# The softmax over the neighbours, computed batch by batch inside the neighbour sum

## What is computed

```
lrelu = lambda h: leaky_relu(h, 0.2)
h = lrelu(_bn(feat @ W1.T, g1, b1))
h = lrelu(_bn(h @ W2.T, g2, b2))
h = lrelu(_bn(h @ W3.T, g3, b3))           # one channel
att = softmax(h[..., 0], axis=-1)          # over K = 30 neighbours
agg = einsum('bnkc,bnk->bnc', x.T[bidx, idx], att)
return x + agg.T
```

## Time and profile before

| | us |
|---|---|
| median of 3 runs | 6674.75 |
| fastest and slowest run | 6666.72, 6677.72 |
| the profiled execution, its own time | 6667.89 |
| its span, first to last instruction | 6665.9 |
| busy: TensorE, VectorE, ScalarE, GpSimd | 5685.7, 5886.1, 4461.5, 3249.3 |
| attention and neighbours | to about 5100 |
| third layer's end to the last softmax operation | 5373.5 to 5422.5 |
| start-up of the neighbour sum | 5422.5 to 5453.2 |
| neighbour sum | 5453.2 to 6665.9 |

### The profile page before, as it was taken

The page is one execution under the profiler, slowest core; times in us unless marked ns, Lnnn a source line. Parts: engine busy times, 40 slices in busy tenths (PEclk is TensorE's granted clock), DMA queues, the critical chain, the costliest instruction groups (busy, mean ns, idle before and its releaser), DMA issues. The chain is left out here.

```text
span 6665.9 us, 228315 instructions
## 1 busy us (share of the span) xinstructions
PE 5685.7 (85%) x83284; PEld 3456.0 (52%) x83284; DVE 5886.1 (88%) x8332; ACT 4461.5 (67%) x17049; POOL 3249.3 (49%) x3279
## 2 busy tenths in 40 slices
PE   7888888888888888888888888888839949999998
PEld 3454545455555545545554555555423337677776
DVE  7999999999999999999999999999946588777776
ACT  7787878787787878787877878788822533333333
POOL 3455655555555555555655555555550023333332
PEclk9999988898888999898898998998859979999999
DMA  2333333233333333333233333333241013333332
GB/s 48 89 97 85 93 91 91 84 91 87 100 92 91 97 85 94 91 90 91 85 92 102 91 91 92 93 91 90 80 118 35 0 38 90 90 83 89 87 84 78
DMA packets 633780, 564.50 MB, mean 85 GB/s; under 512 B 535517, under 2 KB 557277, under 8 KB 598653
## 3 DMA queue, kind: packets, MB, share of 16 engines
q1 hardware_dynamic: 632572, 548.75, 29.1%
HBM read 380.55 MB, written 67.24 MB: 67 GB/s over the span
## 5 line engine op out<-in xcount | busy, mean ns | idle before, releaser
L703 ACT ACTIVATE prob<-SC,row_max 128x64 f32<-128x64 f32 x6144 | 1835.3, 327 | 671.7 <-DVE row_max L1032 664.8
L817 POOL TENSOR_TENSOR prob<-prob,row_rec 128x512 f32<-128x512 f32 x768 | 829.9, 1081 | 1897.7 <-DVE row_rec L1040 1897.1
L703 ACT ACTIVATION_READ_ACCUMULATOR prob<-SC,row_max 128x1 f32 x6144 | 1349.0, 220 | 0.0
L1024 DVE FIND_INDEX8 nbr<-top,dist 128x8 uint16<-128x1024 f32 x1024 | 1235.8, 1220 | 0.0
L1017 DVE MAX8 top<-dist 128x8 f32<-128x1024 f32 x1024 | 1194.1, 1207 | 12.6 <-DVE y_b L1055 10.3
L610 PE MATMUL PT<-ident,prob 128*128 128x128 f32 x3072 | 516.1, 295 | 573.9 <-ACT prob_t L710 563.2
L610 PEld LDWEIGHTS PT<-ident,prob 128*128 128x128 f32 x3072 | 383.6, 151 | 1076.8 <-issue 1033.2
L589 PE MATMUL SC<-k_bd,q_t 128*64 128x256 f32 x6144 | 935.8, 430 | 0.0
L1019 DVE MATCH_REPLACE8 dist<-top,dist 128x1024 f32<-128x1024 f32 x768 | 925.2, 1210 | 0.0
L1816 DVE TENSOR_TENSOR d_oh_a<-lo,iota_a 128x4096 bf16<-128x4096 bf16 x256 | 584.4, 2293 | 255.2 <-PE DM L1667 254.8
L1708 ACT ACTIVATE dense<-DM 128x512 f32<-128x512 f32 x512 | 305.6, 597 | 746.3 <-PE DM L1667 746.1
(11 more groups left out here) (194 smaller groups left out, 9538.6 us busy)
## 6 DMA issues: line engine op xcount, KB each, us to landing
low_all<-low_scratch SPq DMA_DIRECT2D x256, 1024.0 KB, 4.9
k_bd<-k_t SPq DMA_DIRECT2D x3072, 16.0 KB, 1.9
placed<-compact SPq DMA_DIRECT2D x256, 192.0 KB, 3.7
ctx<-in_ctx SPq DMA_DIRECT2D x32, 512.0 KB, 4.0
mask<-in_mask SPq DMA_DIRECT2D x32, 512.0 KB, 7.8
xb<-in_x SPq DMA_DIRECT2D x32, 512.0 KB, 4.3
x_scratch<-xb SPq DMA_DIRECT2D x32, 512.0 KB, 4.7
y_scratch<-y_b SPq DMA_DIRECT2D x32, 512.0 KB, 6.6
```

What stands on the lines that cost most here:

```text
L703: last = act.activation(prob[:, s % 4, g * CHUNK:(g + 1) * CHUNK], SC[:, s % 2, g * CHUNK:(g + 1) * CHUNK], ACT.Exp, bias=row_max[:, s % 2 ...
L817: pool.tensor_tensor(pr, pr, row_rec[:, r % 2, :].unsqueeze(2).to_broadcast([128, 8, CHUNK]), ALU.mult).then_inc(normed, 1)
L1024: last = dve.max_index(nbr[:, uu % BPB, t, k * 8:(k + 1) * 8], best, row)
```

## The change

The softmax leaves `batch_norms`. There GpSimd now lays out the rows, a pair of neighbours at a time behind each transpose of the third layer, without gain and shift; `att` has rows of 30 and `gain3` and `shift3` are kept for the next part. In `neighbour_sum` each batch's rows get their softmax one batch ahead: ScalarE's copy after x = 1 applies gain and shift; VectorE does the leaky ReLU, the maximum and the subtraction at the end of slot 1 (`exponents`); ScalarE does the exponential after x = 5 (`powers`); VectorE does the sum, the reciprocal and the multiply in slot 3, ahead of the transpose (`weights`). In the start-up the memsets of `placed` go behind the transpose (VectorE) and behind the split (GpSimd), and VectorE waits for the constants later.

```
 batch_norms, GpSimd, behind inv2:
+                if n == 1:
+                    by_row = att[:, :, :].rearrange("p (b t) k -> p b t k", t=NT)
+                    for m in range(PAIRS_K):
+                        pool.wait_ge(z3_turned, m + 1)
+                        pool.tensor_copy(by_row[:, :, :, 2 * m:2 * m + 2], S[:, 0, 2 * m:2 * m + 2, :].rearrange("p k (t b) -> p b t k", t=NT)).then_inc(laid_out, 1)
 batch_norms, ScalarE and VectorE: the four-part softmax is taken out
-            for x in range(PARTS_S):
...
+            wait(dve, "gain3")
 neighbour_sum, ScalarE:
-              act.activation(at_n[:, :].rearrange("p (n k) -> p n k", k=KP), keep["att"][:, bass.ds(b(NT), NT), :],
-                               ACT.Identity).then_inc(copied_in, 1)
+              act.activation(at_n[:, :, 0:K], keep["att"][:, bass.ds(b(NT), NT), :], ACT.Identity, scale=keep["gain3"][:, 0:1],
+                               bias=keep["shift3"][:, 0:1]).then_inc(copied_in, 1)
+            def powers(b):
+                act.wait_ge(lowered, START + b(1, 1))
+                act.activation(at_n[:, :, 0:K], at_n[:, :, 0:K], ACT.Exp).then_inc(powered, 1)
...
+                    if x == 5 and not is_last(i, u):
+                        powers(counter(i, u + 1))
 neighbour_sum, GpSimd:
             pool.wait_ge(consts_in, START + 16 * len(CONSTS))
+            split_weights(counter(0, 0), 0, False)
             pool.memset(placed[:, 1, :, :, :, :], 0.0).then_inc(cleared[1], 1)
-            split_weights(counter(0, 0), 0, False)
 neighbour_sum, VectorE:
+            def exponents(b):
+                own, wide = at_n[:, :, 0:K], [128, NT, K]
+                dve.wait_ge(copied_in, START + b(1, 1))
+                dve.scalar_tensor_tensor(own, own, SLOPE, own, ALU.mult, ALU.max).then_inc(leaky, 1)
+                dve.wait_ge(leaky, START + b(1, 1))
+                dve.tensor_reduce(top[:, :], own, AX.X, ALU.max).then_inc(highest, 1)
+                dve.wait_ge(highest, START + b(1, 1))
+                dve.tensor_tensor(own, own, top[:, :].unsqueeze(2).to_broadcast(wide), ALU.subtract).then_inc(lowered, 1)
             def weights(b):
-                dve.wait_ge(copied_in, START + b(1, 1))
+                own, wide = at_n[:, :, 0:K], [128, NT, K]
+                dve.wait_ge(powered, START + b(1, 1))
+                dve.tensor_reduce(total[:, :], own, AX.X, ALU.add).then_inc(scaled, 1)
+                dve.wait_ge(scaled, START + b(3, 1))
+                dve.reciprocal(scale[:, :], total[:, :]).then_inc(scaled, 1)
+                dve.wait_ge(scaled, START + b(3, 2))
+                dve.tensor_tensor(own, own, scale[:, :].unsqueeze(2).to_broadcast(wide), ALU.mult).then_inc(scaled, 1)
+                dve.wait_ge(scaled, START + b(3, 3))
                 dve.wait_ge(at3_ready, START + b(1))
-                dve.transpose(at_t[:, :], at_n[:, :]).then_inc(at_ready, 1)
+                dve.transpose(at_t[:, :], at_n[:, :, :].rearrange("p t k -> p (t k)")).then_inc(at_ready, 1)
...
                     if t == 1 and not is_first(i, u):
                         first_half(i, u - 1)
+                    if t == 1 and not is_last(i, u):
+                        exponents(counter(i, u + 1))
...
+            dve.memset(at_n[:, :, K:KP], 0.0)
+            indices(counter(0, 0), 0, 0)
+            exponents(counter(0, 0))
+            dve.wait_ge(consts_in, START + 16 * len(CONSTS))
+            one_hot_blocks(counter(0, 0))
+            weights(counter(0, 0))
             dve.memset(placed[:, 0, :, :, :, :], 0.0).then_inc(cleared[0], 1)
```

More of the change, by code:

```diff
@@ L1135 @@
 LOADS = (0, 4, 12, 20, K)
-PARTS_S = 4
-SHARE = N * NT // PARTS_S
 BN_ROW = (("W1", 36), ("W2", 18), ("W3", 3), ("g1", 6), ("g2", 3), ("g3", 1), ("b1", 6), ("b2", 3), ("b3", 1))
@@ L1192, in batch_norms @@
         inv = sb("inv", [128, 2])
-        gain = [sb(f"gain{n}", [128, w]) for n, w in ((1, 2), (2, 1), (3, 1))]
-        shift = [sb(f"shift{n}", [128, w]) for n, w in ((1, 2), (2, 1), (3, 1))]
-        top = sb("top", [128, N * NT])
-        total = sb("total", [128, N * NT])
+        gain = [sb(f"gain{n}", [128, w]) for n, w in ((1, 2), (2, 1))] + [keep["gain3"]]
+        shift = [sb(f"shift{n}", [128, w]) for n, w in ((1, 2), (2, 1))] + [keep["shift3"]]
         Z = ps("Z", [128, BANKS, 512])
@@ L1217, in batch_norms @@
         u2_ready = sem("u2_ready")
-        u3_ready = sem("u3_ready")
-        lowered = sem("lowered")
-        powered = sem("powered")
+        laid_out = sem("laid_out")
         block = es.enter_context(nc.Block())
@@ L1352, in _ @@
                     act.activation(kept(w), Z[:, w % BANKS, :], ACT.Identity).then_inc(z3_kept, 1)
-            wait(act, "gain3")
-            act.wait_ge(z3_turned, PAIRS_K)
-            by_row = S[:, 0, :, :].rearrange("p k (t b) -> p b t k", t=NT)
-            for x in range(PARTS_S):
-                mine = att[:, x * SHARE:(x + 1) * SHARE, 0:K].rearrange("p (b t) k -> p b t k", t=NT)
-                share = SHARE // NT
-                act.activation(mine, by_row[:, x * share:(x + 1) * share], ACT.Identity, scale=gain[2][:, 0:1],
-                               bias=shift[2][:, 0:1]).then_inc(u3_ready, 1)
-            for x in range(PARTS_S):
-                mine = att[:, x * SHARE:(x + 1) * SHARE, 0:K]
-                act.wait_ge(lowered, x + 1)
-                act.activation(mine, mine, ACT.Exp).then_inc(powered, 1)
         @block.vector
@@ L1456, in _ @@
             norm(3, st3, 128, 1, given["g3"], given["b3"])
-            wide = [128, SHARE, K]
-            dve.memset(att[:, :, K:KP], 0.0)
-            for x in range(PARTS_S):
-                own = slice(x * SHARE, (x + 1) * SHARE)
-                dve.wait_ge(u3_ready, x + 1)
-                link(dve.scalar_tensor_tensor(att[:, own, 0:K], att[:, own, 0:K], SLOPE, att[:, own, 0:K], ALU.mult, ALU.max))
-                link(dve.tensor_reduce(top[:, own], att[:, own, 0:K], AX.X, ALU.max))
-                dve.tensor_tensor(att[:, own, 0:K], att[:, own, 0:K], top[:, own].unsqueeze(2).to_broadcast(wide), ALU.subtract).then_inc(lowered, 1)
-            for x in range(PARTS_S):
-                own = slice(x * SHARE, (x + 1) * SHARE)
-                dve.wait_ge(powered, x + 1)
-                link(dve.tensor_reduce(total[:, own], att[:, own, 0:K], AX.X, ALU.add))
-                link(dve.reciprocal(total[:, own], total[:, own]))
-                dve.tensor_tensor(att[:, own, 0:K], att[:, own, 0:K], total[:, own].unsqueeze(2).to_broadcast(wide), ALU.mult)
+            wait(dve, "gain3")
 DM_BANKS = 4
@@ L1502, in neighbour_sum @@
         iota_m = sb("iota_m", [128, 8], BF16)
-        at_n = sb("at_n", [128, NT * KP])
+        at_n = sb("at_n", [128, NT, KP])
+        top = sb("top", [128, NT])
+        total = sb("total", [128, NT])
+        scale = sb("scale", [128, NT])
         at_t = sb("at_t", [128, NT * KP])
@@ L1530, in neighbour_sum @@
         at_ready = sem("d_at_ready")
+        leaky = sem("leaky")
+        highest = sem("highest")
+        lowered = sem("lowered")
+        powered = sem("powered")
+        scaled = sem("scaled")
         at3_ready = sem("at3_ready")
@@ L1714, in _ @@
             weights(counter(0, 0))
+            powers(counter(0, 0))
             all_batches(act, body)
@@ L1780, in _ @@
         def _(dve):
-            dve.wait_ge(consts_in, START + 16 * len(CONSTS))
             def indices(b, u, j):
@@ L1878, in body @@
                         compact_blocks(counter(i, u + 1), i, (u + 1) % BPD, t - 6)
+            dve.memset(at_n[:, :, K:KP], 0.0)
[4 more added lines that the diff above has]
+            weights(counter(0, 0))
             dve.memset(placed[:, 0, :, :, :, :], 0.0).then_inc(cleared[0], 1)
-            indices(counter(0, 0), 0, 0)
-            weights(counter(0, 0))
-            one_hot_blocks(counter(0, 0))
             for h in range(2):
@@ L1897, in build @@
         attention_and_neighbours(nc, dram, keep)
-        keep["att"] = es.enter_context(nc.sbuf_tensor("att_all", [128, N * NT, KP], F32))
+        keep["att"] = es.enter_context(nc.sbuf_tensor("att_all", [128, N * NT, K], F32))
+        for name in ("gain3", "shift3"):
+            keep[name] = es.enter_context(nc.sbuf_tensor(name, [128, 1], F32))
         batch_norms(nc, dram, keep)
```

1 line of the change is left out of this document (added).

## The result

The changed kernel takes **6714.29 us** (median of 4 runs, 6710.82 to 6719.0) against 6675.35 for the kernel before (median of 4, 6666.72 to 6677.72). The ratio is 1.0061, 95% interval 1.0048 to 1.0075: slower by more than the 0.2% that can be told apart. The profiled execution took 6710.82 us with a span of 6708.8, which is 42.9 more than the 6665.9 of before.

A forecast was written before the change was run, and what follows sets the result against it. TensorE's pace bounds the neighbour sum; the softmax before it is all on the path. -49.0 - 1.3 + 1 + 70.5 + 3.5 + 15.2 = +39.9 on 6667.89 gives 6707.8, plus 6.9 for the median: 6714; range 6686 to 6746.

The forecast's parts named there:

- the port: Neighbour sum: GpSimd's split, now starting with slot 4's table, meets VectorE's operations; 0.95 us per batch in 16 batches, +15.2 us.
- Softmax removed and batch 0: The softmax stage before the neighbour sum goes, -49.0 us; batch 0 pays 2.2 in slot 1 and about 1.3 more, +3.5.
- Slot 3, the wait: VectorE's softmax rest waits for the exponential behind copy x = 5, delaying slot 4's table; TensorE stands 2.35 us, 30 batches, +70.5.
- the late split: GpSimd's split starts at 6409.5 instead of 6403.76, outside VectorE's gap; 0.95 us of VectorE per batch, hidden in 14, +15.2.
- the rival of the falling clock: TensorE's idle ahead of slot 4 may lower its granted clock; about 1 us per batch, +31, 6745 us; 10%.
- an idle of 2.35 us: TensorE's stand ahead of slot 4 in each batch; may lower the clock as the idle 5.13 us at loop turns did.
- The test written down with the prediction: Sign in the profile after: a clock under 1.00 behind slot 4 means the falling of the clock holds.
- Start-up: Stretch before TensorE's first DM matmul, reordered: 3.9 us later if GpSimd's memset holds the compact products, else 6.5 earlier; -1.3 taken.
- No row has this pair, so I take the middle: Start-up: whether GpSimd's memset holds VectorE's compact products was not in the profile; middle of both bounds taken, -1.3 us.
- Third layer: GpSimd's 15 copies of 512 elements beside VectorE's gapless work, bounds 0 and 19 us; 15 x 0.07 taken, +1.
- the rival of the copies: GpSimd's copies take VectorE's time in the third layer, as the two exclude each other; +17 on the forecast, 6731 us; 9%.
- Faster (6%): Rival: slot 4's stall does not reach TensorE, leaving only the removed softmax stage; 6626 us with nothing getting through; 6%.

## Why the prediction was right

The forecast was 6714.7, given as 6714; the measurement is 6714.29. Its largest terms are right by their own working. Smaller terms were off and compensated, so that the two agree to half a microsecond is luck. The execution in the profile was forecast at 6707.8 and took 6710.82; the start-up came out 4.5 us better than forecast, the port and the clock together 4.7 worse, the part up to the third layer's end 1.8 worse; and the median lies 3.5 above that execution, where 6.9 were added.

**Softmax removed and batch 0.** -49.0 was exact (5373.46 to 5422.45), and batch 0 lost 3.74 us where 3.5 were worked out.

**Slot 3, the wait.** +70.5 forecast. The idle time ahead of slot 4 grew by 73.15 us, 2.34 to 2.51 per batch against 2.35, and the time from slot 3's start to slot 4's by 70.6. A pair of batches got 6.1 us longer, against 5.65. The step that carries it, that the copy x = 5 starts at the very instant at which slot 4's table used to, shows in batch 3 above: copy at 5527.30, table 2.42 us later. Moving the exponential alone took the cost away, and moving a plain copy into that place alone made one like it.

**Port and clock.** The forecast had +15.2 for the late split and nothing for the clock, which was the rival of the falling clock with +31 and 10%. Measured were +3.8 ahead of slot 0 and +16.1 in slow AG products, together 19.9. The mechanism of the late split was right: VectorE's way is 0.9 us longer (0.95 forecast), and without the slow product it costs 17 to 19.5 us. But it is a way beside TensorE's, and TensorE's own got longer at the same time. The step that failed is "an idle of 2.35 us" being left without a cost in the sum. The rival's price for it, 1 us per batch, was too high: it was 0.5 in the product, 0.7 with slot 4's own matmuls. That the sum came out so near owes something to this: two costs of the same size lie side by side, and with the slow product taken away (the two runs with matmuls in the gap) the time was nearly the same. The slow product without the late split was not run. The test written down with the prediction, a granted clock under 1.00 behind slot 4, says that the mechanism of this rival holds, beside the forecast's and not in its place.

**Start-up.** -1.3 forecast, -5.76 measured (30.74 to 24.98). The step that failed is "No row has this pair, so I take the middle": a memset of GpSimd does not hold the compact products. The Trainium skill ("SBUF — State Buffer", Who interferes with whom) had given this end, 5 us earlier than the sum, and here trace and page agree: 3.63 us for six products through the memset, against 8.79 us for a tensor_scalar of 0.23. That second row fits the same section too: it sets the operations that can run in a 2-port mode, tensor_scalar among them, apart as contending with GpSimd. No row here shows in which mode this one ran. Taking the row of a tensor_scalar as a bound for a two-input product was the mistake, and the middle cost 4.5 us.

**Third layer.** +1 forecast, 0 measured. The length of the copy was taken at 1.25 us, and is 1.06, so it fits into the 1.2 us that VectorE's operation leaves free. The rival of the copies (+17, 9%) rests on the same page's rule that such a pair excludes each other. The rule holds by the trace, 3.07 us beside 2.24, and the rival still falls, because exclusion costs only the one that comes second. That too stands in the section, which says that whoever issues first has the ports for its whole instruction; the prediction left it out, and with it the order of the two in time would have been the thing to work out. Only with the copies doubled did VectorE come second pair after pair, and the layer lose 7.7 us.

**Faster (6%).** Nothing of the stall was absorbed, so this fell as worked out. Its time, 6626, is near what the kernel takes (6623.9) once the stall is gone.

**Left open.** The +2.8 us ahead of the third layer are not explained; the last shift stands anywhere between 5373 and 5386 us in the profiles of these kernels, the ones that leave that part alone included. Why the clock falls 1.1 us after TensorE has begun to stand in one batch and 3.6 in another was not settled; the shorter wait's higher price (1.1 to 1.3 us per batch in the product, against 0.5) goes with more of the slow stretch lying on the product, but no run moved that stretch on its own. Nor was it settled why extra matmuls at slot 4 bring issue gaps ahead of the loop's turn, and slow products behind slot 0.

## What to carry to other kernels

When a chain is spread over engines that each have slack, look up for each step the instant at which its input is made and the instant at which the waiting engine's next critical piece is released: here 90 us (6714 against 6624) hung on whether a 0.4 us exponential was queued behind ScalarE's copy 3 or copy 5, and VectorE's share of busy time said nothing of it. A short wait on TensorE is to be priced with what follows it, since the slow product behind it added from a fifth (16.1 on 73.5 us) to nearly the whole (38.0 on 39.9 us) of the wait itself. And a term that lies on one of two parallel ways is paid only as far as it exceeds the other, so two such terms may neither be summed nor removed one by one.

## What the runs showed of the hardware

Three things were not expected.

- An idle time of TensorE of 1.3 us, in the kernel before with its copy behind x = 5, was enough for the granted clock to fall to 0.50 in 30 of 30 batches. The product behind took 4.0 to 5.3 us instead of 3.68, 34.1 us in all. Behind 2.4 us in the changed kernel it took 3.7 to 5.3 us, 16.1 in all. In both the clock fell 1.1 to 3.6 us after TensorE had begun to stand. Where the slow stretch lay on the 96 short DM matmuls it cost at most 0.2 us (2.74 in place of 2.57), where it lay on the product up to 1.6. So the wait and its price in clock are not proportional. With matmuls in the gap the products behind slot 4 were at 3.68 us in all of batches 1 to 30.
- GpSimd's permuted f32 copy of 512 elements took 1.06 us alone and 3.07 with a 2.24 us operation of VectorE ahead of it; where the copy was first, that operation took 3.08. The first ran through and the second paid all of it.
- An f32 matmul with 512 columns stood in the trace as two records, which follow each other every 0.44 us; whoever wants to fill a gap with such matmuls has to count both.
